# A four-layer graph network on one core: wide VectorE operations of two convolutions, a four-head attention and half of a last layer written row by row, or moved to PSUM, TensorE and ScalarE

## The reference, cut to what matters

```python
x = _layernorm(x + _L0_gnn_ref(x, L0_gnn_W, L0_gnn_c, edge_index))
x = _layernorm(x + _L1_gnn_ref(x, src, dst, L1_gnn_W1_1, L1_gnn_W2_1, L1_gnn_W1_2, L1_gnn_W2_2))
x = _layernorm(x + _L2_gnn_ref(x, edge_index, L2_gnn_W, L2_gnn_att_src, L2_gnn_att_dst, L2_gnn_bias))
x = _layernorm(x + _L3_gnn_ref(x, edge_index, edge_attr_16, batch0, L3_gnn_W, L3_gnn_a))

# one convolution of layer 1 (two of them, a relu between)
msg = (h_src @ W1 + h_src * h_dst @ W2) * norm[:, None]
out = x @ W1 + jax.ops.segment_sum(msg, dst, num_segments=n_nodes)

# layer 2, four heads, with self loops
alpha = ex / (seg_sum[dst] + 1e-16)
out = jax.ops.segment_sum(x[src] * alpha[:, :, None], dst, num_segments=N).mean(axis=1) + bias

# layer 3: both directions of each edge and self loops
src, dst = concatenate([src0, dst0, loop]), concatenate([dst0, src0, loop])
logits = leaky_relu(s_node[src] + d_node[dst] + e_all)
att = exp(logits - m[dst]) / denom[dst]
out = jax.ops.segment_sum(att[:, None] * xt[src], dst, num_segments=num_nodes)
```

## Time and profile before

| | us |
|---|---|
| median of 3 runs | 8034.38 |
| lowest, highest | 8027.68, 8039.57 |
| profiled execution, first to last instruction | 8027.0 |
| DVE busy | 5509.6 (69%) |
| POOL busy | 5303.4 (66%) |
| PE busy | 2987.5 (37%) |
| ACT busy | 2914.7 (36%) |

### The profile page before, as it was taken

How to read it: one execution, slowest core, us unless ns; L and a number is a source line. 1 busy time by engine, 2 the same in 40 slices (tenths; PEclk the granted TensorE clock), 3 DMA queues, 4 the chain that set the end, 5 groups by cost and what they waited for, 6 DMA issues and landing times. The chain is left out here.

```text
span 8027.0 us, 77025 instructions
## 1 busy us (share of the span) xinstructions
PE 2987.5 (37%) x14049; PEld 2387.9 (30%) x14049; DVE 5509.6 (69%) x16229; ACT 2914.7 (36%) x6536; POOL 5303.4 (66%) x5145
## 2 busy tenths in 40 slices
PE   4776700211111115766656635454400000263322
PEld 1222200211111115666646634454400000252221
DVE  6667687877767756777779969999734444473764
ACT  3555523433333334444435536666500000121211
POOL 0003773777777767777757737777567777777677
PEclk9888855555555557778856655555555555576555
DMA  9884218111111114555569944444321111663321
GB/s 101 110 117 98 68 18 63 27 26 26 26 25 25 25 39 141 168 163 167 160 212 327 328 159 148 146 151 151 126 62 44 45 45 45 132 226 114 97 91 61
DMA packets 786581, 864.04 MB, mean 108 GB/s; under 512 B 469875, under 2 KB 483427, under 8 KB 779804
## 3 DMA queue, kind: packets, MB, share of 16 engines
q1 hardware_dynamic: 572556, 684.47, 30.9%
q0 software_dynamic: 163408, 175.42, 10.5%
q10 hardware_dynamic: 50240, 0.60, 0.6%
HBM read 419.15 MB, written 480.23 MB: 112 GB/s over the span
## 5 line engine op out<-in xcount | busy, mean ns | idle before, releaser
L164 POOL DMA_INDIRECT T<-slot_at,home_row x393 | 434.4, 1105 | 818.4 <-DVE home_row L728 677.9
L1244 POOL DMA_INDIRECT e_other<-X,index x392 | 428.1, 1092 | 177.3 <-issue 117.4
L1232 POOL DMA_INDIRECT e_ahead<-XA,index x392 | 416.3, 1062 | 178.6 <-issue 118.8
L1892 POOL DMA_INDIRECT e_mine<-T,index x392 | 392.3, 1001 | 206.1 <-issue 114.3
L3012 POOL DMA_INDIRECT e_got<-G,index x392 | 411.6, 1050 | 176.7 <-issue 112.9
L3634 POOL DMA_INDIRECT out_rows<-e4s_out,index x392 | 416.8, 1063 | 165.2 <-issue 118.8
L2383 PE MATMUL e_turned<-ident,e_own_x 128*128 128x128 f32 x196 | 54.6, 434 | 1229.4 <-DVE e_own_x L1971 1229.4
L1904 POOL DMA_INDIRECT X<-e_row,index x392 | 419.0, 1069 | 125.3 <-issue 118.8
L2532 POOL DMA_INDIRECT e_got<-X,index x392 | 413.6, 1055 | 119.5 <-issue 119.5
L2529 POOL DMA_INDIRECT e_mine<-X,index x392 | 404.4, 1032 | 130.4 <-issue 119.2
L3443 POOL DMA_INDIRECT rows<-X,index x392 | 395.6, 1009 | 130.6 <-issue 130.6
(11 more groups left out here) (685 smaller groups left out, 13023.6 us busy)
## 6 DMA issues: line engine op xcount, KB each, us to landing
XA<-e_n_xa SPq DMA_DIRECT2D x49, 1056.0 KB, 5.5
SUMS<-e_state SPq DMA_DIRECT2D x49, 1056.0 KB
e4n_n_xa<-XA SPq DMA_DIRECT2D x49, 1056.0 KB, 5.3
X<-e_n_row SPq DMA_DIRECT2D x49, 576.0 KB
X<-pl_x SPq DMA_DIRECT2D x98, 268.0 KB, 3.0
e_n_x<-X SPq DMA_DIRECT2D x49, 536.0 KB
B<-e_n_b SPq DMA_DIRECT2D x49, 528.0 KB
e_n_b<-B SPq DMA_DIRECT2D x49, 528.0 KB
```

Source lines behind the costliest of these rows:

```text
L164: gp.indirect_dma_start(out=words, out_offset=bass.IndirectOffsetOnAxis(ap=home_row[:, t:t + 1], axis=0), in_=slot_at[:, t:t + 1], in_offs ...
L1232: gp.indirect_dma_start(out=ahead[:, b, j, :], out_offset=None, in_=g.XA[0:SLOTS, :], in_offset=bass.IndirectOffsetOnAxis(ap=index_of(g, 0 ...
L1244: gp.indirect_dma_start(out=other[:, h, j, :], out_offset=None, in_=others[:, :], in_offset=bass.IndirectOffsetOnAxis(ap=index_of(g, s, 1, ...
L1892: gp.indirect_dma_start(out=mine[:, h, j, :], out_offset=None, in_=g.T0[:, :], in_offset=bass.IndirectOffsetOnAxis(ap=index_of(g, s, 0, n, ...
```

## The change

Four stages are touched, and the set-up a little.

- Set-up: a tile `bias_row` on one partition holds the bias twice, padded to the width of a pair of heads.
- First convolution: the payload, scaled_slots, node_g2 and node_x2 become one tensor_scalar per row of 64 columns, with the factor taken per partition (8, 8, 16 and 16 instructions in place of four). The aggregate tile and its wait go; both_parts becomes 16 scalar_tensor_tensor rows that multiply and add, or multiply and multiply. node_bias goes; each product into `heads` is followed by an accumulating product of one row of ones with `bias_row`.
- Second convolution: x2_rows and the node rows become 8 and 16 tensor_scalar rows, the aggregate tile moves to PSUM, the bias operation and its wait go, with the same added products on PE.
- Four heads: joined goes; PE turns z[:, 0] and z[:, 1] with products that accumulate into one place (32 in place of 16), waits for both, and ACT's loop_products waits until PE has read z[:, 1] of the chunk before. The edge share `beta` lies in PSUM. x3_rows becomes 8 rows.
- Destination half: ACT makes the looped product in 8 activations into a double buffer; DVE's three wide operations become 8 scalar_tensor_tensor rows.

```diff
@@ heads and edge, end of a chunk
-                    if end and kind == "heads":
-                        joined(end, J)
...
-                    sums_dve.done(v.tensor_tensor(sent[:, h, 0:count, 0:D], state[:, h, 0:count, 0:D],
-                                                  rise[0].to_broadcast([P, count, D]), ALU.mult), "q0")
-                    sums_dve.done(v.tensor_tensor(looped[:, 0:count, :], x3_own[:, h, 0:count, 2:],
-                                                  rise[1].to_broadcast([P, count, D]), ALU.mult), "q1")
-                    need("q1")
-                    sums_dve.done(v.tensor_tensor(sent[:, h, 0:count, 0:D], sent[:, h, 0:count, 0:D],
-                                                  looped[:, 0:count, :], ALU.add), "a0")
+                    v.wait_ge(loop_made.sem, loop_made.after(n))
+                    for j in range(count):
+                        last = v.scalar_tensor_tensor(out=sent[:, h, j, 0:D], in0=state[:, h, j, 0:D], scalar=logs[:, b, 0, j:j + 1],
+                                                      in1=looped[:, b, j, :], op0=ALU.mult, op1=ALU.add)
+                    sums_dve.done(last, "a0")
...
-                    row_done.done(v.tensor_tensor(row[:, h, 0:count, :], y[:, b, 0:count, :],
-                                                  small[:, 3, 0:count].unsqueeze(2).to_broadcast([P, count, D + 2]), ALU.mult))
+                    for j in range(count):
+                        last = v.tensor_scalar(row[:, h, j, :], y[:, b, j, :], small[:, 3, j:j + 1], None, ALU.mult)
+                    row_done.done(last)
...
+                    if not (isinstance(n, int) and n < 1):
+                        a.wait_ge(end_pe.sem, end_pe.after(n - 1, "z3"))
...
-                    t.wait_ge(end_dve.sem, end_dve.after(n, "z"))
+                    t.wait_ge(end_dve.sem, end_dve.after(n, "z0"))
+                    t.wait_ge(loop_made.sem, loop_made.after(n))
...
-                            last = t.transpose(z_turned[:, 4 * i + r, :], z[:, 0, j, q * P:(q + 1) * P], g.ident[:, :])
+                            for a in range(2):
+                                last = t.matmul(z_turned[:, 4 * i + r, :], lhsT=z[:, a, j, q * P:(q + 1) * P], rhs=g.ident[:, :], start=(a == 0), stop=(a == 1))
@@ first convolution
-                    acc.done(v.tensor_tensor(pay[:, :, 0:D], got[:, h, :, 0:D], got[:, h, :, D:D + 1].to_broadcast([P, J, D]), ALU.mult), "pay")
+                    for j in range(J):
+                        paid = v.tensor_scalar(pay[:, j, 0:D], got[:, h, j, 0:D], got[:, h, j, D:D + 1], None, ALU.mult)
+                    acc.done(paid, "pay")
...
-                    v.tensor_tensor(both[:, b, 0:count, 0:D], agg[:, 0:count, :], x, ALU.add)
-                    sums.done(v.tensor_tensor(both[:, b, 0:count, D:], agg[:, 0:count, :], x, ALU.mult), "u1")
+                    for j in range(count):
+                        for half, op in ((slice(0, D), ALU.add), (slice(D, 2 * D), ALU.mult)):
+                            last = v.scalar_tensor_tensor(out=both[:, b, j, half], in0=state[:, h, j, 0:D], scalar=g.rsi[:, bass.ds(n * J + j, 1)],
+                                                          in1=x[:, j, :], op0=ALU.mult, op1=op)
+                    sums.done(last, "u1")
...
-                    b2_done.done(v.tensor_tensor(rows, rows, g.bias[:, :].unsqueeze(1).to_broadcast([P, 2 * GROUP, D + 2]), ALU.add))
...
-                            last = t.matmul(heads[:, i // 2, (i % 2) * 2 * (D + 10):(i % 2 + 1) * 2 * (D + 10)], lhsT=x2_t[:, q, i, :],
-                                            rhs=g.w2_pair[:, :, :].rearrange("p a k -> p (a k)"), start=True, stop=True)
+                            pair = heads[:, i // 2, (i % 2) * 2 * (D + 10):(i % 2 + 1) * 2 * (D + 10)]
+                            t.matmul(pair, lhsT=x2_t[:, q, i, :], rhs=g.w2_pair[:, :, :].rearrange("p a k -> p (a k)"), start=True, stop=False)
+                            last = t.matmul(pair, lhsT=g.ones[0:1, :], rhs=g.bias_row[:, :, :].rearrange("p a k -> p (a k)"), start=False, stop=True)
@@ second convolution
-        result, carried = ps("result", [P, J, D]), ps("carried", [P, D])
+        result, carried, agg = ps("result", [P, J, D]), ps("carried", [P, D]), ps("agg", [P, J, D])
...
-                    v.wait_ge(close.sem, close.after(n, "row"))
-                    close.done(v.tensor_tensor(b2[:, h, :, :], b2[:, h, :, :], g.bias[:, :].unsqueeze(1).to_broadcast([P, J, D + 2]), ALU.add), "b2")
+                    close.done(v.tensor_copy(halves[1][:, :, :, 0:2], part[:, :, :, 8:10]), "b2")
```

More of the change, by code:

```diff
@@ L1683, in own_rows @@
                     logs_exp.done(a.activation(logs[:, b, :, 0:count], logs[:, b, :, 0:count], ACT.Exp))
+                    a.wait_ge(logs_exp.sem, logs_exp.after(n))
+                    if begun(c, 2):
+                        a.wait_ge(sums_dve.sem, sums_dve.after(n - 2, "a0"))
+                    for j in range(count):
+                        last = a.activation(looped[:, b, j, :], x3_own[:, h, j, 2:], ACT.Copy, scale=logs[:, b, 1, j:j + 1])
+                    loop_made.done(last)
                 def attend(c):
@@ L2491, in body @@
                         n, b = c5.n, c5.slot % 2
[L2492 removed]
+                        sp.wait_ge(b_made.sem, b_made.after(n, 1))
                         sp.nop(nofuse=True)
@@ L2630, in scaled_slots @@
                     v.wait_ge(g2_kept[h], c.k * 16)
-                    g2_made.done(v.tensor_tensor(g2_slot[:, h, :, :], xh[:, h, :, D:],
-                                                 g.rso[:, bass.ds(n * J, J)].unsqueeze(2).to_broadcast([P, J, D]), ALU.mult))
+                    for j in range(J):
+                        last = v.tensor_scalar(g2_slot[:, h, j, :], xh[:, h, j, D:], g.rso[:, bass.ds(n * J + j, 1)], None, ALU.mult)
+                    g2_made.done(last)
                 def node_spread(c):
@@ L2652, in node_g2 @@
                     v.wait_ge(g2_stored[b], (c.k * 2 + h // 2) * 16)
-                    g2_done.done(v.tensor_tensor(both_flat(g2[:, b, :, :, :]), both_flat(h1[:, b, :, :, :]),
-                                                 both_flat(x1[:, h, :, :, D:D + 1]).to_broadcast([P, 2 * GROUP, D]), ALU.mult))
+                    for q in range(2):
+                        for j in range(GROUP):
+                            last = v.tensor_scalar(g2[:, b, q, j, :], h1[:, b, q, j, :], x1[:, h, q, j, D:D + 1], None, ALU.mult)
+                    g2_done.done(last)
                 def node_x2(c):
@@ L2662, in node_x2 @@
                         v.wait_ge(row_copied.sem, row_copied.after(n - 2))
-                    x2_made.done(v.tensor_tensor(both_flat(x2_c[:, b, :, :, :]), both_flat(y[:, b, :, :, :]),
-                                                 small[:, 3, :, :].rearrange("p q j -> p (q j)").unsqueeze(2).to_broadcast([P, 2 * GROUP, D]), ALU.mult))
+                    for q in range(2):
+                        for j in range(GROUP):
+                            last = v.tensor_scalar(x2_c[:, b, q, j, :], y[:, b, q, j, :], small[:, 3, q, j:j + 1], None, ALU.mult)
+                    x2_made.done(last)
                 def node_y(c, q):
@@ L3114, in x2_rows @@
                         v.wait_ge(row_copied.sem, row_copied.after(n - 2))
-                    x2_made.done(v.tensor_tensor(x2_c[:, b, 0:count, :], y[:, b, 0:count, :],
-                                                 small[:, 3, 0:count].unsqueeze(2).to_broadcast([P, count, D]), ALU.mult))
+                    for j in range(count):
+                        last = v.tensor_scalar(x2_c[:, b, j, :], y[:, b, j, :], small[:, 3, j:j + 1], None, ALU.mult)
+                    x2_made.done(last)
                 def closing(c, count):
@@ L3153, in node_x3 @@
                     v.wait_ge(n_stored[h], c.k * 16)
-                    x3_made.done(v.tensor_tensor(both_flat(n_row[:, h, :, :, :]), both_flat(n_b2[:, h, :, :, :]),
-                                                 n_small[:, 3, :, :].rearrange("p q j -> p (q j)").unsqueeze(2).to_broadcast([P, 2 * GROUP, D + 2]), ALU.mult))
+                    for q in range(2):
+                        for j in range(GROUP):
+                            last = v.tensor_scalar(n_row[:, h, q, j, :], n_b2[:, h, q, j, :], n_small[:, 3, q, j:j + 1], None, ALU.mult)
+                    x3_made.done(last)
                 def node_scores(c):
@@ L3310, in head_products @@
                     for i in range(GROUP // 2):
[L3311 to L3312 removed]
+                        pair = heads[:, i // 2, (i % 2) * 2 * (D + 10):(i % 2 + 1) * 2 * (D + 10)]
+                        t.matmul(pair, lhsT=x2_t[:, i, :], rhs=g.w2_pair[:, :, :].rearrange("p a k -> p (a k)"), start=True, stop=False)
+                        last = t.matmul(pair, lhsT=g.ones[0:1, :], rhs=g.bias_row[:, :, :].rearrange("p a k -> p (a k)"), start=False, stop=True)
                     m3.done(last)
```

71 lines of the change are left out of this document (28 added, 43 removed).

## The result

| | us |
|---|---|
| before, median (8027.68 to 8039.57) | 8033.76 |
| changed, median of 4 (8365.71 to 8390.0) | 8381.98 |
| ratio, 95% interval | 1.0434 (1.042 to 1.0449) |
| profiled execution of the changed kernel, span | 8363.8 |

The account below looks back on a forecast made before the run. POOL was taken to bound the first convolution loosely, DVE the second convolution and four heads, POOL's transfers the destination half. Set-up +1, +169, +73, -82, -12 sum to +149 on 8034: 8183 us, range 8040 to 8290.

Parts of the forecast that it names:

- PE's added products: First convolution: four more accumulating products of 148 columns per group put +1.11 us on the cycle.
- upper bound: First convolution: the added products cost at most 2.34 us, the time of the same group after a long idle.
- the signs of being wrong: Rows at 0.13 us or below, added products much under 1.1, or the first convolution's turn staying at POOL's 20 to 21.5.
- Second convolution: Rows +2.24 us, bias and wait gone -0.74, added products hidden: +1.50 a chunk, +73 us; bounds +30 to +107.
- The rows: DVE's new 64-column rows: 0.167 us per tensor_scalar row, 0.196 per two-input row.
- Cheap rows: Rival: rows start every 0.13 us and the first convolution's quiet turn is 17.4, total 7980 us; chance 0.17.
- The cycle: First convolution: DVE, PE, ACT, DVE grows from 18.9 to 25.0 us, above POOL's 19.9; stage +169 us.
- The rival with POOL held up by the rows: Each row shuts POOL out while it runs: first convolution +311 us, total 8377 us; chance 0.05.
- PE slow: Rival: longer idle puts the first convolution's new products at the lower clock, +60 us; chance 0.20 shared with heads giving little.
- Four heads: Joining operations go, output rows added: DVE falls from 20.2 to 18.5 us a chunk, PE's turning 7.3 hidden; -82 us.
- Destination half: POOL's 392 scatters average 998 ns against 940, at most 23 us to be had; half of it, -12 us.
- The 7 us around the span: Profiled span 8027.0 against median 8034.4: 7 us taken to lie around the span, so the sum is added to the median.

Follow-up runs that it names:

- the run with the tall weight: Changed kernel with the bias row zero-padded to 128 partitions and a 128-row weight of ones, same products and columns: 8201.2 us.
- The 64- and 32-row runs: Changed kernel with the bias row and its weight of ones 64 or 32 rows tall instead of one: 8377.1 and 8378.9 us.
- the bias on DVE: Changed kernel with both convolutions' bias added on VectorE again, no bias-row products on PE, all rows kept: 8164.9 us.
- the one-row products ahead: Changed kernel with two one-row bias products of 296 columns ahead of the four others instead of between them: 8261.2 us.
- the run with the aggregate alone: Kernel before plus the change's attention parts, with the second convolution's aggregate tile moved from SBUF to PSUM: 7957.9 us.

## Why the prediction was wrong

The direction and most terms were right; one term of the sum, PE's added products, was mis-sized, and the time fell out of the range because that term's upper bound was no bound.

- **The step that failed**: "The present four need 1.11 until the transforms follow ... I take +1.11, with 2.34 as the upper and nothing as the lower bound, since only the moving columns are known to be equal." The four added products cost +2.4 us at the full clock and +4.2 at the lower, 3.1 on average over both groups of a chunk (4.53 - 1.40), and +3.8 in the second half's group, the one on the cycle (5.47 - 1.71). I had priced a product by its columns from a row in which all weights have one height; the bias row's weight has another, and no row shown of before has two heights in turn. The upper bound was the same price at the lower clock, and the signs of being wrong name only products that take less than 1.1. In the run with the tall weight that price nearly holds (+0.9 at the full clock, +2.0 at the lower); it ends at 8201, 18 us from the forecast and within its range. The 64- and 32-row runs tie the rest to the change of height. With the growth of the second half's group in the place of the 1.11, the prediction's sum (18.9 + 5.0 and the growth) gives a turn of 24.3 us with the bias on DVE (measured 24.2), 26.0 with tall weights (25.6), 26.5 with the one-row products ahead (26.3) and 27.7 in the change (27.6).
- **Second convolution**: "with double the products they need 2.29 more, while DVE's new rows move that point 2.24 later, so the 0.6 of slack hardly changes and hides them." The group grew by 3.9 (6.2 for 2.3 on average) and the cover was too thin by a part of that; DVE waits 24.3 us in 38 turns for it (4480 to 5010). With tall weights the stage is +71, for +73 forecast:

```profile
DVE e_b L3132 <- PE e_heads L3318: 24.3, 26, 1.2
...
4711.69 3.01 DVE L3159 TENSOR_SCALAR e_n_row<-e_n_b,e_n_small 128x66 f32<-128x66 f32 x16
...
4718.33 1.97 PE L3294 MATMUL e_turned<-ident,e_both 128*128 128x128 f32 x8
4718.43 0.69 DVE L3132 TENSOR_TENSOR e_b<-e_x_c,e_heads 128x512 f32<-128x512 f32 x1 [0.91 <-PE e_heads L3318]
```

  Besides, "The aggregate in PSUM costs DVE the same columns" missed the 0.23 us by which the aggregate ends late in 33 of 49 chunks.
- **The rows** were priced right: 0.168 for 0.167, 0.196 for 0.196; +120 and +109 us of stage for +115 and +109 once PE's products are out. *Cheap rows* is refuted.
- **The cycle** DVE, PE, ACT, DVE as the first convolution's new bound was right: 24.2 us without the products for 23.9, 25.6 with tall ones for 25.0. In the kernel before, too, POOL was the bound as said, and fully: 637 us of transfers and 611 issues of 0.30 fill the 823 us.
- **The rival with POOL held up by the rows** names nearly the measured time, 8377, by chance: POOL's transfers got shorter beside the rows (964 ns for 1055), and POOL is busy for 609 of 1100 us in the stage that it was to bound. **PE slow** was the rival in the right place; its price, 60 us, was less than half of the 140 by which the first convolution ran over (309 - 169), and its reason, the clock alone, accounts for about 19 of them at most, which is what is left with tall weights (188 - 169).
- **Four heads** -89 for -82: right in mechanism and size; but the price of PE's turning, "twice the products are 7.3", was too low (10.3), and its cover was nearly used up.
- **Destination half** -4 for -12: "average 998 ns against 940" sets a scatter against a gather's time. A scatter takes 973 ns in the median and 971 at least before, and the same now, so the stretch was 25 ns and not 58, 10 us in all. Half of it went, 13 ns each: the share was right, the stretch that it was taken of was not.
- **The 7 us around the span**: in the runs after it a time is 2 us above its own span, so most of the 7 lies between executions. The sum doesn't hang on it.

## What to carry to other kernels

Price an added matrix product by its neighbours, not by its columns: a weight of another height between tall ones holds back the weight loads on both sides, so pad it to the same height, or put such products together in a pause of PE. A bound for an unseen cost must come from a row that differs in the same way as the new instruction does; the widest price of a like one is no upper end. Of an engine that stands on a cycle, price the group that the cycle waits for, at the clock that it has there, and not the mean of all groups; and where the engine stands in a turn twice, count both places, even where only one of them is waited for today.

## What the runs showed of the hardware

- A product whose weight has another height than its neighbours' (128 rows next to 1, 32 or 64) takes 0.45 us at the full clock and 0.79 at the lower; in the group with equal heights it is 0.25 and about 0.5. Two one-row products of 296 columns after one another take 1.19 us, four tall ones of 148 columns 1.11.
- In a series, a 64-column row with a scalar per partition takes 0.168 us and a two-input one 0.196, the latter also where each row waits for the one before, as in the chain of the earlier trace rows.
- POOL's transfers beside DVE's operations (overlapping by over 0.1 us, first convolution): before, all 94 beside both_parts, 512 columns wide with two inputs in SBUF, take over 1.0 us, 1.25 on average; of 67 beside the sums y, as wide but with one input in PSUM, none does. In the changed kernel 50 of the 143 beside the two-input rows of both_parts do, none over 1.08; of 329 beside rows with a scalar alone 13 do, none over 1.02. The Trainium skill ("SBUF — State Buffer", Who interferes with whom) says that an operation with two inputs in SBUF contends with what GpSimd reads there, and one with a single such input, outside the two-port modes, doesn't; the trace agrees (the gathers' indices lie in SBUF). The same section infers that a tensor_tensor doesn't stall GpSimd's descriptors, and lets a tensor_scalar in a two-port mode shut GpSimd out for the whole instruction; the transfers beside both_parts and beside the rows show neither. Whether the rows run in a two-port mode, no run shows.
- In the second convolution, in the changed kernel and in the run with the aggregate alone, some operations of DVE ended about 0.2 us late; all of these began 0.47 to 0.64 us after the start of a transfer, though not all that began then were late. Why stays open.
